# Two-layer transformer: the routing of three sequences of the second mixture moves from its own stage into the units of the second attention

## The reference

```
x = x + attn0(norm(x))       # 16 heads of 64, causal, scores clamped by 50 tanh(s / 50)
x = x + moe0(norm(x))        # 8 experts, the best one for each token
x = x + attn1(norm(x))       # 16 heads of 8 from a latent of 64, rope, causal by pages of 32
n = norm(x)
x = x + moe1(n) + shared(n)  # 8 gated experts, the best two for each token, and one shared expert
```

## Time and profile before

| | |
|---|---|
| median of three runs | 2032.82 us (2029.81 to 2037.74) |
| the profiled execution | 2018.03 us, span 2016.3 us |
| PE, DVE, ACT, POOL busy | 87, 68, 60, 25% of the span |
| second attention's units (window 1147.5 to 1634) | 486.5 us |
| `dispatch`, with the barriers around it (1663 to 1818) | 155 us |
| `expert_tiles` (1818 to 1981) | 163 us |

### The profile page before, as it was taken

The page is one execution under the profiler, slowest core; times in us unless marked ns, Lnnn a source line. Parts: engine busy times, 40 slices in busy tenths (PEclk is TensorE's granted clock), DMA queues, the critical chain, the costliest instruction groups (busy, mean ns, idle before and its releaser), DMA issues. The chain is left out here.

```text
span 2016.3 us, 38324 instructions
## 1 busy us (share of the span) xinstructions
PE 1753.2 (87%) x12164; PEld 1047.7 (52%) x12164; DVE 1373.3 (68%) x2900; ACT 1219.2 (60%) x1726; POOL 510.0 (25%) x816
## 2 busy tenths in 40 slices
PE   5999999999999999975954799899989986668992
PEld 3566555655565556545932233333333325438992
DVE  6677777777677777764566788787878834445665
ACT  5888888788878888843654166565656672213441
POOL 0222211232124212303422012121212222363441
PEclk9999999999999999987977599998999995888996
DMA  5201111111101111113234312131313103011224
GB/s 176 61 29 31 38 37 38 37 46 37 38 28 41 38 38 38 37 67 94 62 117 150 105 31 60 32 58 34 59 32 57 34 2 126 28 53 52 61 60 138
DMA packets 101207, 115.90 MB, mean 57 GB/s; under 512 B 15467, under 2 KB 75212, under 8 KB 100397
## 3 DMA queue, kind: packets, MB, share of 16 engines
q1 hardware_dynamic: 90294, 98.12, 18.1%
q0 software_dynamic: 6592, 13.56, 2.0%
q10 hardware_dynamic: 4160, 2.10, 0.4%
HBM read 78.86 MB, written 34.41 MB: 56 GB/s over the span
## 5 line engine op out<-in xcount | busy, mean ns | idle before, releaser
L1493 ACT ACTIVATE a_p<-a_score 128x1024 f32<-128x1024 f32 (+3 forms) x384 | 300.8, 810 | 227.6 <-PE a_score L1510 223.7
L1598 DVE TENSOR_REDUCE a_mx<-a_misc 128x1 f32<-128x512 f32 (+3 forms) x768 | 377.2, 549 | 67.8 <-PE a_misc L1541 46.6
L306 ACT ACTIVATE a_p<-a_score 128x1024 f32<-128x1024 f32 (+3 forms) x384 | 292.8, 816 | 40.8 <-PE a_score L343 39.5
L1538 PE MATMUL a_misc<-a_k,a_q 72*128 72x512 bf16 (+3 forms) x768 | 254.3, 352 | 50.3 <-DVE a_out L1675 22.9
L248 POOL TENSOR_SCALAR_AFFINE_SELECT a_p<-a_p 128x256 f32<-128x256 f32 x256 | 130.0, 537 | 647.1 <-ACT a_p L324 647.1
L324 ACT ACTIVATE a_p<-a_p 128x2560 f32<-128x2560 f32 (+1 forms) x128 | 273.8, 2139 | 1.1
L343 PE MATMUL a_score<-a_q,a_k 64*128 64x512 f32 (+3 forms) x2304 | 269.4, 364 | 3.7 <-ACT a_p L306 2.0
L362 PE MATMUL a_out<-a_p,a_v 128*64 128x512 f32 (+3 forms) x1536 | 269.8, 493 | 0.0
L1510 PE MATMUL a_score<-a_q,a_k 128*128 128x512 bf16 (+3 forms) x768 | 234.6, 332 | 1.9 <-ACT a_p L1493 1.6
L343 PEld LDWEIGHTS a_score<-a_q,a_k 64*128 64x128 f32 x2304 | 186.7, 188 | 86.9 <-issue 41.3
L522 DVE TENSOR_TENSOR a_part<-a_part,a_p 128x1024 f32<-128x1024 f32 (+3 forms) x256 | 223.7, 874 | 7.8 <-ACT a_p L324 1.2
(11 more groups left out here) (278 smaller groups left out, 2669.4 us busy)
## 6 DMA issues: line engine op xcount, KB each, us to landing
a_xt<-xt SPq DMA_DIRECT2D x31, 512.0 KB
a_q<-qk_parts SPq DMA_DIRECT2D x144, 64.0 KB
a_k<-qk_parts SPq DMA_DIRECT2D x144, 64.0 KB
e_xs<-f_x_rows SPq DMA_DIRECT2D x110, 64.5 KB, 1.8
qk_parts<-p_part SPq DMA_DIRECT2D x24, 256.0 KB, 4.9
xt<-a_p SPq DMA_DIRECT2D x9, 512.0 KB, 3.6
a_w<-in_l_attn_w SPq DMA_DIRECT2D x32, 128.0 KB, 3.0
values<-p_values SPq DMA_DIRECT2D x4, 1024.0 KB, 6.1
```

The lines of the kernel that those rows point to most:

```text
L306: nc.scalar.activation(chunk_of(prob[p], c), score_ps[:, c % 2, :, 0:width], ACT.Tanh, scale=scale / clamp).then_inc(tanh_done, 1)
L1493: nc.scalar.activation(prob[s % RING][:, :, 0:width], score_ps[:, s % 2, :, 0:width], ACT.Exp, scale=scale).then_inc(exp_done, 1)
L1538: mm = nc.tensor.matmul(misc[:, bank, 0:keys], q_st[bn][0:ROWS, h, t * P:(t + 1) * P], k_st[bn][0:ROWS, h, key0:key0 + keys], start=True, ...
L1598: nc.vector.tensor_reduce(m[c][:, h, t:t + 1], misc[:, bank, 0:keys], AX_X, ALU.max).then_inc(free, 1)
```

## The change

Class `Routes2` takes the steps that `dispatch` did for a sequence. For the first three sequences `attention1` does them in slots of the four units that follow the sequence's last one:

- unit 0 of the four: `heads` turned in slots 19 and 20 and copied out by DVE (before: by ACT), projection by `wo` in slots 21 and 22 and added to `x`;
- unit 1: statistics in slots 0 to 8, square root by ACT in slot 11, normalisation in slots 14 to 23;
- unit 2: turned in slots 3 and 4 and copied out by DVE, gate in slot 8, the 11 choosing steps in slots 10 to 20, doubling by ACT in slot 5;
- unit 3: rank in slot 2, placing in slots 4 to 6, on POOL 8 scatters behind the mask of slot 7 and one behind each mask of slots 16 to 23.

The transposes, projection, gate and rank are uses of the ring of three banks. `steps` no longer has a loop: all 18 steps are written out. `dispatch_last2` replaces `dispatch`: it routes the fourth sequence and computes all 8 blocks of the shared expert. In `attention0` each step behind the statistics comes one unit later, and the normalisation goes to the end of DVE's list of its unit. To make room, the normalised rows lie in tiles of the projection stage, and its `values` in `xt_all`.

```diff
@@ attention0
-                if i == 8 and at in (1, 2):
-                    routes.act_turned(act, b, at - 1, spare)
+                if i == 8 and at in (2, 3):
+                    routes.act_turned(act, b, at - 2, spare)
...
                     dve_r_low(dve, m)
-                    if at == 1:
-                        routes.dve_normed(dve, b)
...
             if at == 0:
                 dve.wait_ge(x_added[1], before + 1)
                 routes.dve_statistics(dve, b)
-            elif at == 3:
+            elif at == 1:
+                routes.dve_normed(dve, b)
+            elif at == 4:
                 routes.dve_choose(dve, b)
@@ attention1
+        ROUTED = {0: {19: ("heads", 0), 20: ("heads", 1), 21: ("attend", 0), 22: ("attend", 1)},
+                  2: {3: ("turn", 0), 4: ("turn", 1), 8: ("gate", None)}, 3: {2: ("rank", None)}}
...
+        def routed(u):
...
+            b, at = divmod(u - QUADS, QUADS)
+            return (b, at) if 0 <= b < BATCH - 1 else (None, None)
...
+            b, step = routed(u)
+            for s, (what, half) in ROUTED.get(step, {}).items():
+                by_slot[s].append((what, (b, half), None))
...
+                    if step == 3:
+                        if slot == 7:
+                            for entry in range(TILES):
+                                routes.pool_scatter(pool, b, entry)
+                        elif slot >= 16:
+                            routes.pool_scatter(pool, b, TILES + slot - 16)
...
+                if step == 1 and s == 11:
+                    routes.act_deviation(act, b)
+                elif step == 2 and s == 5:
+                    routes.act_doubled(act, b)
...
+            elif kind == "heads":
+                b, half = arg
+                pe.wait_ge(free, number_of(u, "turn_out", 1) + 1)
+                mm = routes.pe_heads(pe, b, half, whole)
+            elif kind == "attend":
+                b, half = arg
+                pe.wait_ge(free, number_of(u, "heads", arg) + 1)
+                mm = routes.pe_attend(pe, half, heads_t, whole)
...
+            elif kind == "heads":
...
+                nc.vector.tensor_copy(heads_t[:, half * HALF:(half + 1) * HALF], whole).then_inc(free, 1)
+            elif kind == "attend":
+                rows = routes.dve_rows(*arg)
+                nc.vector.tensor_tensor(rows, rows, whole.rearrange("p (t d) -> p t d", d=D), ALU.add).then_inc(free, 1)
...
+        def dve_routing(dve, u, s):
...
+            b, step = routed(u)
+            if step == 1:
...
+                if s < TILES:
+                    routes.dve_statistics(dve, b, s)
+                elif s == TILES:
+                    routes.dve_moments(dve, b)
+                elif s == 14:
+                    routes.dve_inverse(dve, b)
+                elif 15 <= s < 15 + TILES:
+                    routes.dve_normed(dve, b, s - 15)
...
+            elif step == 2 and 10 <= s < 10 + routes.CHOOSING:
...
+                routes.dve_choose(dve, b, s - 10)
+            elif step == 3 and 4 <= s < 4 + routes.PLACING:
...
+                routes.dve_place(dve, b, s - 4)
...
-            for u in (-1, 0):
-                plain(u)
-            looped = (UNITS - BUFS) // BUFS
-            with eng.Fori(0, looped) as it:
-                for i in range(BUFS):
-                    step(eng, it * BUFS + (1 + i), (1 + i) % BUFS, lambda k, i=i: it + (1 + i + k) // BUFS)
-            for u in range(1 + looped * BUFS, UNITS + 1):
+            for u in range(-1, UNITS + 1):
                 plain(u)
@@ dispatch_last2, TensorE and VectorE
+                for half in range(2):
+                    routes.pe_heads(pe, last, half, bank[half][:]).then_inc(heads_turned, 1)
+                for half in range(2):
+                    pe.wait_ge(heads_out, half + 1)
+                    routes.pe_attend(pe, half, heads_t, bank[half][:]).then_inc(projected, 1)
+                blocks(0, 1)
+                for half in range(2):
+                    pe.wait_ge(attended, half + 1)
+                    routes.pe_turn(pe, last, half, bank[half][:]).then_inc(turned, 1)
+                pe.wait_ge(xt_out, 2)
+                routes.pe_gating(pe, last, bank[0][:]).then_inc(gated, 1)
+                blocks(1, 2)
+                routes.pe_rank(pe, last, bank[1][:]).then_inc(ranked, 1)
+                blocks(2, BLOCKS)
...
+                blocks(2, 3)
+                tile_table()
+                V.tensor_tensor(ex[:], routes.logits[:], wide(top[0][:], [P, ALL_TILES, E]), ALU.subtract).then_inc(exp_in, 1)
+                V.tensor_tensor(top[1][:], top[1][:], top[0][:], ALU.subtract).then_inc(exp_in, 1)
+                blocks(3, BLOCKS)
```

More of the change, by code:

```diff
@@ L1755, in dispatch @@
     SLOT_TILES = PACK * tile_expert.shape[1]
-    FAR = -3e38
     BLANKS = E + SPARE
     x_flat = x_rows.rearrange("n p d -> (n p) d")
+    last = BATCH - 1
+    BLOCKS = TOKENS // HALF
     with ExitStack() as ctx:
         k = kit.scope(ctx)
-        gate = k.sb(f"{tag}_gate", [P, E])
-        biases = 0 if bias_dram is None else bias_dram.shape[1]
-        bias = k.sb(f"{tag}_bias", [P, max(biases, 1), E])
-        numbers = k.sb(f"{tag}_numbers", [P, ALL_TILES + N])
+        routes.xn[last] = [k.sb(f"{tag}_xn{c}", [P, TILES, D + 1]) for c in range(2)]
+        heads_t = k.sb(f"{tag}_heads_t", [P, SEQ])
+        ex = k.sb(f"{tag}_ex", [P, ALL_TILES, E])
+        top = routes.top
@@ L1772, in dispatch @@
-        xt = xt_all if xt_all is not None else k.sb(f"{tag}_xt", [P, TOKENS])
-        logits = k.sb(f"{tag}_logits", [P, ALL_TILES, E])
-        top = [k.sb(f"{tag}_top{c}", [P, ALL_TILES]) for c in range(choices)]
-        shape = [P, TILES, E]
-        at_max, left = k.sb(f"{tag}_at_max", shape), k.sb(f"{tag}_left", shape)
-        first = k.sb(f"{tag}_first", [P, TILES])
-        number = k.sb(f"{tag}_number", [P, 1, E])
-        one = [k.sb(f"{tag}_one{i}", [P, COLS + 1, E], BF16) for i in range(2)]
@@ L1815, in turns_before @@
[L1815 to L1828 removed]
+        passed, jumped = (k.sb(f"{tag}_{n}", [1, SLOT_TILES, E]) for n in ("passed", "jumped"))
@@ L1857, in _ @@
             def _(pool):
-                nc.gpsimd.memset(full[:], 1.0).then_inc(made, 1)
-                pool.wait_ge(made, 1)
-                nc.gpsimd.affine_select(out=below[:], in_=full[:], compare_op=ALU.is_gt, fill=0.0, base=0,
-                                        pattern=[[1, P]], channel_multiplier=-1).then_inc(made, 1)
-                for i in range(2):
-                    nc.gpsimd.memset(one[i][:, COLS:, :], 0.0).then_inc(made, 1)
-                nc.gpsimd.memset(blank[:], 0.0).then_inc(blank_made, 1)
@@ L2000, in _, with blocks @@
-                if choices == 2:
-                    act.wait_ge(exp_in, 2)
-                    nc.scalar.activation(ex[:], ex[:], ACT.Exp).then_inc(exp_done, 1)
-                    nc.scalar.activation(top[1][:], top[1][:], ACT.Exp).then_inc(exp_done, 1)
+                def blocks(first, end):
+                    for n in range(first, end):
+                        shared.act_up(act, n)
+                for half in range(2):
+                    act.wait_ge(heads_turned, half + 1)
+                    nc.scalar.copy(heads_t[:, half * HALF:(half + 1) * HALF], bank[half][:]).then_inc(heads_out, 1)
@@ new lines, in _ @@
+                flat = blank[:].rearrange("p n d -> p (n d)")
+                nc.scalar.copy(flat, routes.one[:, COLS, 0:1].to_broadcast(flat.shape)).then_inc(blank_made, 1)
+                routes.act_deviation(act, last)
+                blocks(0, 1)
+                act.wait_ge(blank_made, 1)
+                nc.scalar.copy(blank[:, :, D], routes.numbers[:, ALL_TILES:ALL_TILES + BLANKS]).then_inc(blank_made, 1)
+                for half in range(2):
+                    act.wait_ge(turned, half + 1)
+                    at = last * SEQ + half * HALF
+                    nc.scalar.copy(routes.xt_all[:, at:at + HALF], bank[half][:]).then_inc(xt_out, 1)
@@ L2005, in _ @@
+                routes.act_doubled(act, last)
+                blocks(1, BLOCKS)
+                act.wait_ge(exp_in, 2)
+                nc.scalar.activation(ex[:], ex[:], ACT.Exp).then_inc(exp_done, 1)
+                nc.scalar.activation(top[1][:], top[1][:], ACT.Exp).then_inc(exp_done, 1)
             @block.vector
@@ L2155, in _ @@
-                if choices == 2:
-                    shares()
+                for half in range(2):
+                    rows = routes.dve_rows(last, half)
+                    dve.wait_ge(projected, half + 1)
+                    V.tensor_tensor(rows, rows, bank[half][:].rearrange("p (t d) -> p t d", d=D), ALU.add).then_inc(attended, 1)
+                dve.wait_ge(attended, 2)
+                for t in range(TILES):
+                    routes.dve_statistics(dve, last, t)
+                routes.dve_moments(dve, last)
@@ L2435, in ffn @@
```

(8 more changed lines are left out.)

637 lines of the change are left out of this document (305 added, 332 removed).

## The result

| | before | changed |
|---|---|---|
| time, us (median, lowest to highest) | 2031.32 (2023.63 to 2037.74) | 1947.26 (1943.71 to 1950.35) |
| profiled execution / its span | 2018.03 / 2016.3 | 1950.35 / 1948.6 |
| mean granted clock | 0.924 | 0.943 |
| first attention's last mark of POOL L238 | 812.65 | 802.33 |
| first mark of the second attention | 1142.54 | 1131.74 |

The ratio is 0.9584, 95% interval [0.9554, 0.9614]: 84 us less. Each part of the change acted in the direction that I had said, but four terms of the sum promised too little, and one of them rested on a wrong premise: that units written out are 30.96 apart.

What follows compares the result with a forecast made beforehand. It saw PE and DVE nearly full in the second attention, low-clock hand-overs in the routing's stretch, and code waits at loop jumps. -23.6 + 47.6 - 69 - 6 = -51, from 2032.8 to 1982; 8-in-10 range 1955 to 2010.

Steps and rivals of the forecast that it cites:

- The loop goes: Second attention: writing out its loop removes three jumps back and the units then show none of their cost, -23.6 us.
- The first attention: First attention: normalisation behind DVE's sums gives 3.0 twice and 1.5, less 1.5 for scatters; net -6, bounds 0 and -7.5.
- What the units get: Second attention's units: routing three sequences there adds 14.8, 14.8 and 18.0, together +47.6 us, bounds 27 and 81.6.
- The stretch: Routing's own stretch behind the second attention: PE's list ends at 1743.9 instead of 1812.9, -69 us; -74 at full clock.
- its cover: Routing's stretch: DVE's chains lie beside block 0, choosing beside block 1, POOL's scatters off the path; failing that, -62.
- The base: Whole kernel: the profiled 2018.0 lies 14.8 below the median; the same difference was taken from 2032.8, giving 1982.
- the slots swallow more: Rival, second attention's units: routing there costs +27 in place of +47.6, total 1961; chance 0.15.
- they swallow nothing: Rival, second attention's units: all added work counts in full, +81.6, so only -17 overall, 2016; chance 0.14.
- Slow scatters: Rival, POOL in the second attention: a scatter takes 2.02 + 0.30, so only -25 overall, 2008; chance 0.06.
- the loop's time not got back: Rival, second attention: as much code must still be fetched, so only -27 overall, 2005; chance 0.04.
- starved engines: Rival, second attention: every written-out unit stalls for its code, 123 us on top, +72 overall, 2105; chance 0.03.

Runs made afterwards that it cites:

- b_one_place: Kernel before, loop kept, every unit's heads written to the same fixed columns; no total time given, marks 30.11 and 30.10 apart in the loop, 40.15 at a jump.
- the kernel with two parts: Kernel before with the second attention's loop written out and the changed first attention, routing not moved: 1978.2 beside 2018.3, ratio 0.9797; 1983.5 on the other chip.
- b_first_attention: Kernel before with only the whole first attention of the changed kernel put in: 2018.9 beside 2028.7, ratio 0.9944.
- the version with both additions: Changed kernel with the inverse root on GpSimd and the third sequence's scatters behind the barrier: 1926.1 beside 2022.2, ratio 0.9529; 1931.9 beside 2029.9, ratio 0.9522.

## Why the prediction was wrong, step by step

- **The loop goes: -23.6, measured -34.6 and -35.** This is the step that failed most. The jumps were right. But I took 30.96 as the spacing of units written out; the earlier trace rows 1537.97 and 1568.93 stand in the loop too, since a mark belongs to the unit before the one it serves. What the runs show in its place is 30.10, and that the 0.86 are DVE's writes to register addresses (b_one_place). The profile of before hardly shows a unit free of the loop's own cost, and I didn't ask what DVE's addresses cost in it, although the gaps of 0.22 and 0.52 ahead of its heads could be seen.
- **The first attention: -6, measured -9.8 and -11.8.** The normalisation gave 6.2 to 7.6, and I had counted 7.5. But I said that turns, gate and rank move and cost the same. The unit of the choice is 28.6 in most executions of before and 27.07 in most where it stands now, 1.56 less in each of two sequences; the execution that I read had it at 27.1 by chance. Nor does any run show the 1.5 that I counted against, for the scatters in the last unit.
- **What the units get: +47.6.** From two executions of the kernel with two parts (485.5 and 488.8 from the first mark to the last heads) to three of the changed one (535.3, 529.9, 530.7) it is +44.8; against all four executions with the attention written out it is +40. The sum was near, its parts less so, and errors of both signs cancel: unit 1 costs 6.2 to 7.8 instead of 4.8 for the square root's sake, unit 0 2.1 instead of 3.0, unit 3 1.0 instead of 1.5 + 1.3 for POOL, and the third sequence 22 instead of 18.0.
- **The stretch: -69.** From the last heads to the last weight it was 150.9 and is 82.7: -68.2. That step was right, with its cover. Counted from PE's start behind the barrier to its first expert matmul it is 82.9 (some 87 forecast), and the clock from the heads on is 0.86. What I left out is what follows it. Before, POOL still scattered until 1810.57 while DVE ended at 1812.93, POOL waits for its scatters to land ahead of the barrier, and the first expert operation of DVE waited 5.66 us there; now POOL is through at 1721 and the wait is 1.36. That is another -4.3.
- **The base.** I scaled from one execution that lay 14.8 below its median as if the difference were carried over unchanged. It was not only an offset: that execution had cheaper units than the others (the same code took 519.5 and 524.9 in the second attention of two kernels). Its jumps were not cheaper: the three spacings with one are 116.5 together, and 116.3 in b_first_attention.

The misses are -11 (loop), -6 (first attention), -3 (units) and -4 (hand-over), less 1 that the stretch gave too little: some -23 of the -29 on one chip. The other 6 are within the intervals of the steps. The size of the whole miss moves with the kernel before: 84 less in the first measurement, 80 on the one chip, 70 on the other, where the miss is 19 and not 29. The kernel before lay at 2018.3 and 2022.2 on that chip and at 2028.7 and 2029.9 on the other, while the changed one stayed within 1947.3 to 1949.8. Why is open. It is not the jumps of the second attention, as far as one execution on each chip tells: 38.01, 38.26 and 40.15 on the chip where before is faster (b_one_place), 38.34, 39.93 and 38.00 on the other (b_first_attention). Nor is it the loop alone, since the version with both additions moved too, 1926.1 and 1931.9, the same way.

Of the rivals, "the slots swallow more" (1961) named the right direction for a wrong reason: the units cost 40 to 45, not 27. That they swallow nothing, 81.6, is refuted by the same number. Slow scatters, the loop's time not got back and starved engines are refuted too: 0.98 a scatter, -35, and plain units of 30.10.

## What to carry to other kernels

Before a loop is valued by its jumps, compare one of its units with the same unit in straight code, or, where there is none, look on every engine for small gaps ahead of operations whose address comes from a register. An engine that stands off the path (POOL here) can still hold two things, the last chunks of a stage and the barrier behind it: count its work up to both. And a table switch on ACT between two buffers of scores is not half hidden, as I had it: of its 2.9 us at least 2.0 passed, and up to 3.6 a unit were lost; a few small operations on an idle engine cost nothing that could be seen.

## What the chip showed that I had not expected

- Four multiplications that write to a register's address take DVE 0.5 to 1.2 us longer, with the reciprocal ahead of them, than to a fixed one (1.19, 1.50, 1.55 or 1.9 against 0.69).
- Behind the second attention PE started 5.2 us after POOL's last scatter, in every version with a scatter at its end, though no list waits there for it to land; without one it started 1.3 us after DVE.
- GpSimd's operations of 128x8 take 0.20 to 0.24 us and follow each other every 0.29, beside DVE's reductions.
- Unit spacings lie on steps of some 1.5 to 2 us: unit 1 was 34.27, 36.29 or 37.9 and hardly ever between, unit 2 33.81 or 35.35; in the first attention the unit of the choice is 27.07 or 28.63, that of the normalisation 27.5 or 29.0. So small costs can vanish or count double. I have no cause for it.
